# Attention and FP8 feed-forward block: a slot table in place of staged iterations, with row maxima led by half a batch and shift rows sent in quarters

## What is computed

```python
B, T, D, H = 8 batches, 512 rows, 256 columns, 16 heads of 16
xn = layernorm(x)
Q, K, V = xn @ W_q.T, xn @ W_k.T, xn @ W_v.T
Q, K = rope(Q), rope(K)
scores = einsum('bhqd,bhkd->bhqk', Q, K) * 16 ** -0.5     # causal mask
heads = einsum('bhqk,bhkd->bhqd', softmax(scores), V)
attn = heads.reshape(b, t, d) @ W_o.T
xq, wq = fake_quant_fp8(xn), fake_quant_fp8(weight)       # one scale for each tensor
out = x + attn + (einsum('bsd,od->bso', xq, wq) + bias)
```

## Time and profile before

| | us |
|---|---|
| median of 3 runs (467.94 to 469.84) | 468.45 |
| the profiled execution | 468.62 |
| its span from first to last instruction | 466.9 |
| PE busy (share of the span) | 405.5 (87%) |
| DVE busy | 350.1 (75%) |
| ACT busy | 277.3 (59%) |
| POOL busy | 274.4 (59%) |
| mean granted TensorE clock | 0.938 |

### The profile page before, as it was taken

How to read it: one execution, slowest core, us unless ns; L and a number is a source line. 1 busy time by engine, 2 the same in 40 slices (tenths; PEclk the granted TensorE clock), 3 DMA queues, 4 the chain that set the end, 5 groups by cost and what they waited for, 6 DMA issues and landing times.

```text
span 466.9 us, 9145 instructions
## 1 busy us (share of the span) xinstructions
PE 405.5 (87%) x2819; PEld 222.8 (48%) x2819; DVE 350.1 (75%) x1340; ACT 277.3 (59%) x500; POOL 274.4 (59%) x278
## 2 busy tenths in 40 slices
PE   1790676999889999999999999999999999998975
PEld 1440521364345556654565556555655545643443
DVE  3779899969769977997799778977897878842041
ACT  2742932147765677567666765677567656675850
POOL 2304376636746984698459844985498337226552
PEclk9996555599999999999999999999999999999999
DMA  7826747300483238422851375037504760020021
GB/s 234 257 87 197 159 136 193 81 5 18 143 214 84 69 101 204 131 69 78 216 144 46 93 213 152 32 110 206 158 18 124 194 170 2 4 93 3 1 91 46
DMA packets 37617, 53.43 MB, mean 114 GB/s; under 512 B 5152, under 2 KB 31136, under 8 KB 37536
## 3 DMA queue, kind: packets, MB, share of 16 engines
q1 hardware_dynamic: 37568, 52.84, 40.6%
HBM read 35.78 MB, written 17.04 MB: 113 GB/s over the span
## 4 chain that ended last, share of the span: by engine, by line
PE 44%; POOL 22%; ACT 11%; issue 10%; DVE 8%; DMA 3%; POOLq 1%; SPq 1%; ACTq 0%; DVEq 0%
PE st_ps L842 10%; PE o_ps L922 9%; PE s_ps L860 7%; ACT prob L722 6%; PE m_ps L894 5%; PE m_ps L869 4%; POOL prob L427 4%; POOL rot L259 4%; PE m_ps L798 4%; POOL rot L253 3%; DVE scratch L587 3%; POOL xq L457 3%; POOL parts L263 3%; POOL rot L252 2%; POOL qv L453 2%
## 5 line engine op out<-in xcount | busy, mean ns | idle before, releaser
L587 DVE CUSTOM_DVE_ANT_0 scratch<-s_ps,causal 128x512 bf16<-128x512 f32 (+3 forms) x512 | 220.9, 485 | 55.0 <-PE s_ps L860 52.9
L722 ACT ACTIVATE prob<-st_ps 128x512 f32<-128x512 f32 x320 | 174.8, 600 | 97.9 <-PE st_ps L842 97.4
L427 POOL TENSOR_SCALAR_AFFINE_SELECT prob<-prob 128x512 f32<-128x512 f32 (+1 forms) x160 | 86.4, 544 | 130.9 <-ACT prob L722 129.4
L860 PE MATMUL s_ps<-k_st,q_st 96*128 96x512 bf16 (+3 forms) x512 | 130.8, 320 | 7.0 <-DVE rowmax L587 3.2
L842 PE MATMUL st_ps<-q_st,k_st 98*128 98x128 bf16 (+3 forms) x512 | 121.9, 303 | 4.2 <-ACT prob L722 2.8
L922 PE MATMUL o_ps<-prob,v_sb 128*17 128x512 f32 (+3 forms) x1024 | 87.4, 437 | 10.0 <-ACT heads L737 5.1
L842 PEld LDWEIGHTS st_ps<-q_st,k_st 98*128 98x128 bf16 x512 | 42.0, 97 | 76.3 <-ACT prob L722 42.3
L860 PEld LDWEIGHTS s_ps<-k_st,q_st 96*128 96x128 bf16 x512 | 48.9, 99 | 43.7 <-DVE rowmax L587 20.6
L922 PEld LDWEIGHTS o_ps<-prob,v_sb 128*17 128x17 f32 x1024 | 20.5, 96 | 48.3 <-issue 36.0
L587 DVE DVE_READ_ACCUMULATOR2_ANT rowmax<- 128x1 f32 x512 | 41.7, 81 | 0.1
L894 PE MATMUL m_ps<-wo_sb,attnT 128*128 128x256 f32 x128 | 33.2, 381 | 1.8 <-DVE x_res L610 1.4
(11 more groups left out here) (99 smaller groups left out, 502.6 us busy)
## 6 DMA issues: line engine op xcount, KB each, us to landing
qk_parts<-parts SPq DMA_DIRECT2D x16, 768.0 KB, 3.7
q_st<-qk_parts SPq DMA_DIRECT2D x32, 192.0 KB, 3.3
k_st<-qk_parts SPq DMA_DIRECT2D x32, 192.0 KB, 3.7
q_st<-x_dram SPq DMA_DIRECT2D x8, 512.0 KB, 5.5
q_st<-qk_parts SPq DMA_DIRECT2D x32, 128.0 KB, 3.4
k_st<-qk_parts SPq DMA_DIRECT2D x32, 128.0 KB, 3.7
x_res<-x_dram SPq DMA_DIRECT2D x8, 512.0 KB, 3.5
out_dram<-x_res SPq DMA_DIRECT2D x8, 512.0 KB, 4.8
```

The lines of the kernel that those rows point to most:

```text
L427: eng.affine_select(out=ap, in_=ap, compare_op=ALU.is_ge, fill=0.0, base=0, pattern=pat, channel_multiplier=-1).then_inc(masked, 1)
L587: eng.tensor_tensor_reduce(scratch[:, at, col:col + w], s_ps[at][:, col:col + w], causal[:, T - w:T], 1.0, NEG, ALU.add, ALU.max, rowmax[: ...
L722: eng.activation(prob[u][:, half * T:(half + 1) * T], st_ps[ST_BANK[2 * s + half]][:, :], ACT.Exp, scale=SCALE).then_inc(exp_done, 1)
L860: mm = eng.matmul(bank[:, col:col + (qb + 1) * P], q_st[0:ROWS, 1 - par, h, qb * P:(qb + 1) * P], k_st[0:ROWS, 1 - par, h, 0:(qb + 1) * P] ...
```

## The change

The iterations with their stages are replaced by one loop over slots from -10 to 175, which each engine walks with offsets of its own. Batch n has its exponents in slots 20n to 20n + 19 and its maxima ten slots ahead of them, where it was twenty. The list `MISC` becomes the dictionary `OFFSETS` (projections of batch n at slots 20n - 30, -28, -26 and -24, outputs from 20n + 23 to 20n + 34). Each piece of the shift rows now covers one group of four heads: four `shift_rows` for a batch, due in slots 0, 5, 10 and 15. The input is loaded into `xnT` itself and normalised there, in place. Before slot -10 only batch 0 is projected; batch 1 is projected, and batches 3 to 7 are turned, in slots -10 to -4. The last store goes out in four pieces.

```diff
-MISC = [(0, "mt", 1), (0, "v", 0), (1, "qk", 0), (2, "qk", 1), (3, "v", 1), (4, "qk", 2), (5, "o", 0),
-        (6, "o", 1), (6, "qk", 3), (7, "o", 2), (8, "o", 3), (9, "at", 0), (10, "at", 1), (11, "mt", 0),
...
+LEAD = 10
+OFFSETS = {("v", 0): 0, ("mt", 1): 1, ("v", 1): 2, ("o", 0): 23, ("o", 1): 24, ("o", 2): 25, ("mt", 2): 6, ("o", 3): 26,
+           ("at", 0): 26, ("at", 1): 27, ("fin", 0): 28, ("at", 2): 29, ("fin", 1): 30, ("qk", 0): -30, ("mt", 3): 11,
+           ("at", 3): 31, ("fin", 2): 32, ("qk", 1): -28, ("qk", 2): -26, ("fin", 3): 34, ("qk", 3): -24, ("mt", 0): -4}
...
+def quant_slot(n):
+
+    return 23 if n == 0 else SLOTS * n + 16
...
-        turn_ps = [[st_ps[0], st_ps[1]], [s_ps[2], o_ps]]
+        turn_ps = (st_ps[0], o_ps)
...
         @block.sync
...
-            def iteration(b, par, stages, before):
-                if 3 in stages:
-                    shift_rows(b, par, 1)
...
-                if 1 in stages:
-                    query_stacks(b + 2, par, 3 in stages)
-                if 2 in stages:
-                    shift_rows(b + 1, 1 - par, 0)
-                if 1 in stages:
-                    key_stacks(b + 2, par, 3 in stages)
...
+            def shift_rows(n, g):
+
+                c = NG * n + g
+                eng.wait_ge(shift_done, c + 1)
+                eng.dma_start(shift_dram[c % 2].rearrange("t a n -> a t n"), shift[:, :, :])\
+                   .then_inc(shift_out[c % 2], 16)
+                eng.wait_ge(shift_out[c % 2], 16 * (c // 2 + 1))
+                eng.dma_start(q_st[ROWS:ROWS + SHIFT, n % 2, g * HG:(g + 1) * HG, :],
...
+            for slot in range(FIRST_SLOT, END_SLOT):
+                for off, g in ((-3, 0), (2, 1), (7, 2), (12, 3)):
+                    n = batch_at(slot, off)
+                    if n is not None:
+                        shift_rows(n, g)
+                n = batch_at(slot, -22, 1)
+                if n is not None:
+                    query_stacks(n)
+                n = batch_at(slot, -17, 1)
+                if n is not None:
+                    key_stacks(n)
+                n = batch_at(slot, 37 - SLOTS)
+                if n is not None and n > 0:
+                    store(n - 1)
+                n = batch_at(slot, 21)
+                if n is not None:
+                    load_residual(n)
...
         @block.gpsimd
...
-                        if s in (7, 13):
-                            low(eng, n, s // 13)
-                        if s in (3, 8):
-                            rotate(eng, n, s // 8)
-                        if s in (5, 10):
-                            remainder(eng, n, s // 10)
...
+            remainder(eng, 0, 0)
+            invert(2)
+            low(eng, 0, 0)
...
+                for off, step, w in ((-27, rotate, 0), (-25, remainder, 0), (-23, low, 0),
+                                     (-22, rotate, 1), (-20, remainder, 1), (-18, low, 1)):
...
+                for n in quant_at(slot, 2):
...
+                for n in quant_at(slot, 4):
...
         @block.tensor
...
-                    if u == 0 and g % 2 == 0:
-                        eng.wait_ge(shift_in[g // 2], 16 * (b + 1))
...
+                if u == 0:
+                    c = NG * n + g
+                    eng.wait_ge(shift_in[c % 2], 16 * (c // 2 + 1))
```

More of the change, by code:

```diff
@@ L231, in attention_ffn_block @@
         reader = {"qk": (roped, 4), "v": (v_copied, 2), "o": (normed, 4), "at": (at_copied, 4),
[L232 to L239, removed]
+                  "fin": (fin_done, 4), "mt": (shift_done, 4)}
@@ L470, in _ @@
+            nw = NC * D
+            invert(0)
+            invert(1)
+            eng.wait_ge(ln_rstd, 4)
+            fill_ones(0)
+            eng.wait_ge(consts, 7)
+            remainder(eng, 0, 0)
+            invert(2)
+            low(eng, 0, 0)
+            split_weights(0)
+            split_weights(1)
+            split_x(1)
+            for n in range(3, 7):
+                invert(n)
             eng.memset(v_sb[:, :, :, :], 1.0).then_inc(consts, 1)
[L471 removed]
@@ new lines, in high_x, with exp @@
+            def high_x(n):
+                wait_past(eng, full["qk"], 4 * n if n > 1 else 0)
+                eng.copy(x_parts[:, 0], xnT[:, n]).then_inc(x_high, 1)
+            def exp(n, s):
+                g, u = divmod(s, 5)
+                if n > 0 or g > 0:
+                    eng.wait_ge(pv_done, 12 * n + 3 * (g - 1) + (1, 1, 2, 2, 3)[u])
+                for half in range(2):
+                    eng.wait_ge(st_full, 2 * (SLOTS * n + s) + half + 1)
+                    eng.activation(prob[u][:, half * T:(half + 1) * T], st_ps[ST_BANK[2 * s + half]][:, :],
+                                   ACT.Exp, scale=SCALE).then_inc(exp_done, 1)
@@ L974, in _, with scores @@
-            run(iteration)
+            def scores(n, s, between):
+                g, u = divmod(s, 5)
+                if u == 0:
+                    c = NG * n + g
+                    eng.wait_ge(shift_in[c % 2], 16 * (c // 2 + 1))
+                for half in range(2):
+                    i = 2 * s + half
+                    wait_past(eng, exp_done, HALVES * n + ST_BEFORE[i] + 1)
+                    for j, kb, col in unit_parts(u, half):
+                        h = g * HG + j
+                        mm = eng.matmul(st_ps[ST_BANK[i]][:, col:col + T - kb * P],
+                                        k_st[0:ROWS + SHIFT, n % 2, h, kb * P:(kb + 1) * P],
+                                        q_st[0:ROWS + SHIFT, n % 2, h, kb * P:T], start=True, stop=True)
+                    mm.then_inc(st_full, 1)
+                    if half == 0:
+                        between()
```

954 lines of the change are left out of this document (454 added, 500 removed).

## The result

The changed kernel takes **548.09 us** (median of 4 runs, 546.63 to 549.61), the kernel before 468.6 beside it (467.94 to 469.84): a ratio of **1.169, 95% interval 1.164 to 1.174**. The prediction was 534 with a range of 486 to 552 and 0.88 for slower. The profiled execution is one of 549.61 with a span of 547.9.

A forecast was written before the change was run, and what follows sets the result against it. PE bound full batches before; now a wait loop through POOL and SP: slot 10 of batch 0 at 105, batch 1 at 159, five loops of 59.5 to 456.5, end 532.5, plus 1.7: 534 us, range 486 to 552.

The forecast's parts named there:

- The start: Before slot 0: less work ahead of PE's first maximum, slot 0 at 75 against 89.8, a gain of about 15 us.
- The loop: Chain from PE's slot 10 through POOL's `low`, SP's key reads and the third quarter to the next slot 10: 59.5 us.
- (g): PE's clock: each batch restarts at half speed after the wait, costing half of up to 5.7 us, taken as 1.9.
- (c): POOL's ordered work from `low` through rotation, `qv`, remainder, `xq` and the keys' `low`, with five masks: 16.7 us.
- (e): Third quarter's first hop, SBUF to DRAM, directly behind 18 reads: 4.8 us, with 1.4 as bound.
- (f): Third quarter's second hop, DRAM to `q_st`: taken as 2.0 us, with bounds 1.4 and 4.8.
- Hidden wait: Rival: the third quarter lands before PE reaches slot 10, so batches keep their pace: 454 us, chance 0.10.
- Short first hop: Rival: the third quarter's first hop takes 2.0 instead of 4.8, loop 56.7: 514 us, chance 0.12.
- POOL keeps up: Rival: POOL starts the keys' `low` 33 us after slot 10 instead of 40.7, loop 52: 489 us, chance 0.10.
- Clock stays up: Rival: PE's clock stays up in stalls of 8 us, saving 1.9 seven times: 521 us, chance 0.07.
- Late start: Rival: the start isn't earlier than 85, as slots -9 to -5 chain ACT, PE and POOL: 544 us, chance 0.05.
- The signs I named: Seven PE waits for shift rows of 5 us or more, half clock after each, one SP chain, slot 0 near 75.

The follow-up runs named there:

- the cure: Changed kernel with the third quarter of the shift rows sent after the first six key reads instead of behind all 18: 492.65 us, ratio 1.049.
- the best version: Changed kernel plus third quarter between reads, later quantised input, turn and ACT key rounding, some largest values ahead of slot -10, batch 0's input sooner: 464.8 us, 0.992.

## Why the prediction was right

The path, step by step: what I had, and what the changed kernel has.

| point | predicted | measured |
| --- | --- | --- |
| first maximum (slot -10) | 47 | 46.98 |
| slot 0 | 75 | 70.30 |
| slot 10 of batch 0 | 105 | 99.92 |
| slot 10 of batch 1 | 159 | 160.59 |
| slot 10 of batch 6 | 456.5 | 468.02 |
| slot 10 of batch 7 | 501 | 514.31 |
| end of the span | 532.5 | 547.9 |

**The start** was right in kind and 4.7 us too long. From slot -10 to slot 0 it took 23.3, not 28. I had charged ACT's 3.2 us to each of five slots, 16 us; it took 12.2, from 52.17 to the end of the last copy at 64.34, since the first two of the five batches were normalised before slot -10:

```profile
39.30 4.04 ACT L667 ACTIVATE xnT<-xnT,shift_x,rstd 128x256 f32<-128x256 f32 x8 [2.07 <-POOL shift_x L417]
52.17 0.59 ACT L674 COPY xnT<-st_ps 128x512 f32<-128x512 f32 x1 [8.83 <-PE o_ps L788]
...
63.75 0.59 ACT L674 COPY xnT<-o_ps 128x512 f32<-128x512 f32 x1
```

```profile
47.00:70.30 23.30, 18.24 (x98) 12.02 (x98) 19.63 (x79) 12.92 (x24) 11.88 (x9) 0.92 0.36 78
```

PE's clock was also higher (0.92 in this window) than the 0.50 at which the maxima of batch 0 ran before; what that gave isn't shown. The gain is 19.5 us on 89.80.

**The loop** closed where I said, at slot 10, through the same engines in the same order:

| step | predicted | measured |
| --- | --- | --- |
| (a) and (g): PE slots 10 to 16, with the clock | 20.1 + 1.9 | 22.99 |
| (b) to POOL's `low` | 2.0 | 2.35 |
| (c) POOL | 16.7 | 17.33 |
| (d) key write, 18 reads | 3.7 + 8.2 | 4.31 + 8.24 |
| (e) first hop | 4.8 | 4.96 |
| (f) second hop | 2.0 | 1.50 |
| sum | 59.5 | 61.68 |

The choice that mattered was (e). The one row with a shift transfer behind 18 reads the earlier trace rows was taken over the quiet one, and it was right to 0.2; (f) was right to be near the quiet end. SP's hop is 1.35 with a quiet queue, 3.1 behind 6 reads and 4.96 behind 18, and what is in flight decides. The 2.0 us that the Trainium skill (DMA: Bandwidth & Descriptors, Anatomy of one DMA) gives for GpSimd's path would have made 514, and is none of these three.

**Mis-sized terms.** The clock (g): I had 1.9 of a possible 5.7 / 2. The first matmul after each of the seven waits in slot 10 takes 0.61, where the same one takes 0.38 at 70.30, so the clock was down after every one. The clock stays at its lower level from before PE's restart at 345.38 until 351, and slot 10 takes 7.37 (283.70 to 291.07) for 0.89 + 1.08 + 1.49 + 0.99 = 4.45 of work at full clock, 2.9 more: the bound itself. The denser load didn't raise it sooner. With the key write (4.3 for 3.7), POOL (0.6) and slot 17 (0.35), less 0.5 for the second hop, that is the 2.2 of this turn; the five turns together were 9.9 over.

The turn from batch 0 to 1 was put at 54 and took 60.67. It closed over the same chain, and 5.1 of the 6.7 stand in POOL's stretch, from the queries' `low` at 122.74 to the end of the keys' at 142.32: 19.6, where the prediction's terms give 14.5. POOL waited there for exponents ahead of two masks, 2.13 us at 130.27 and 3.25 at 134.15:

```profile
134.15 0.41 POOL L446 TENSOR_SCALAR_AFFINE_SELECT prob<-prob 128x256 f32<-128x256 f32 x1 [3.25 <-ACT prob L697]
```

ACT in its turn waited 3.84 us for PE's scores ahead of 128.71, and PE had stopped twice for the largest values, ahead of 123.20 and 125.84 (1.75 and 1.07), with its clock at 0.66 from 125 to 130. ACT also had the weights' scaling in front of the next exponents (three steps from 130.00 to 132.07). I had costed that batch by what POOL leaves out, and overlooked what waits for the largest values, of which DVE takes three in this turn and five before it; how the 5.1 divides between PE's stops and ACT isn't settled. The rest is in the first two steps of the chain, 22.8 to the start of POOL's stretch, where the prediction's terms give 20.8; the second hop was 0.5 shorter than I had it.

From slot 10 of batch 6 to slot 10 of batch 7 it took 46.3 for 44.5, and from there to the end 33.6 for 31.5: 3.9 more.

So an error below (5.1 us by slot 10 of batch 0, nearly all of it at the start) and three above (6.7, 9.9, 3.9) make +15.4. That they offset is luck: with the start as I had it, the same loop would have ended near 553, just past the range.

**The rivals.** *Hidden wait*: fell; PE waited 44.8 us. *Short first hop*: fell at 4.96. *POOL keeps up*: fell; the keys' `low` starts 40.5 after slot 10 (283.70 to 324.23), where I had 40.7 and the rival 33. *Clock stays up*: fell at 0.50. *Late start*: fell; slot 0 stands at 70.30.

**The signs I named** stood in the profile, with two differences of size: six waits of the seven are over 5 us and the one of batch 1 is 2.82; slot 0 is at 70.3 and not 75.

What I hadn't seen is what the cure showed. With the loop open a batch in the middle of the run still took 52.4, then 48.6, then 47.9, each time for an order of two steps within one engine's queue (DVE's maxima behind the quantised input, a turn behind a bank, exponents behind a rounding). Of the 19.5 us gained at the start, 4 are left in the best version. Its profile (span 460.5 against 466.9) shows where the rest went, counted from slot 0 of a batch to slot 0 of the next: batch 0 takes 47.7 for 42.7 before, batches 1 to 5 together 4.1 more than before, batch 6 44.3 for 41.4, and from slot 0 of batch 7 to the end it takes 56.3 for 54.9. So two thirds of it go in batch 0 and from batch 6 on, outside the full batches. In batch 7 the changed order has ten slots of maxima and the kernel before none; what batches 0 and 6 are made of wasn't tested.

## What to carry to other kernels

A wait moved into a queue is late by all that stands ahead, and where what stands ahead depends on the waiting engine, the lateness repeats each round: follow the chain until it comes back to its start, sum it, and compare with the engine's own period. A small transfer that an engine waits for belongs ahead of bulk reads or between them; giving it another engine's queue gave 16.5 us of the 79 here, and moving it ahead of 12 of the reads gave 55. When work ahead of a phase goes, see what ran under its cover: here eight reductions of DVE turned up in the next phase.

## What the runs showed of the hardware

- **A small DMA behind bulk reads** ends about when they have drained. In the changed kernel the first hop (issued 338.92) ends at 343.88, with the DMA share at 0.82 in 341 to 343 and at 0.00 after; 1.16 us of further issues ahead moved its end by 0.6 only. From another engine's queue it took 4.1 as well.
- **A VectorE step beside a GpSimd step** takes 2.57 us in the version with the third quarter between the reads, and 2.58 in four of eight batches of the changed kernel; in the kernel before all eight take 0.68 to 0.70 (row below). It ends 0.55 after the other's end, so it seems to have waited for nearly all of it. The Trainium skill (SBUF — State Buffer, Who interferes with whom) says that `tensor_scalar` can take the port pair that VectorE shares with GpSimd, and that whichever comes second blocks for the whole instruction. These rows agree, and they have GpSimd first by 0.11.

```profile
L640 DVE TENSOR_SCALAR qe<-qv x8: 683/684/695, 141.8 to 449.4; 128x1024 uint32<-128x1024 uint32 x8
```

- **TensorE's clock** fell to its lower level some 2 us after PE stopped (338.92, and 0.51 in 341 to 343) and came back some 6 us after PE restarted (345.38, and 0.85 in 351 to 352), though PE was busy nearly all of that time. A stop of 2.70 us was enough for a fall in the version with the third quarter between the reads, when PE was back at work already:

```profile
280.00:283.00 3.00, 0.30 (x4) 0.21 (x3) 2.97 (x7) 0.80 (x2) 3.00 (x3) 1.00 1.00 333
283.00:287.00 4.00, 3.91 (x13) 2.52 (x11) 2.99 (x16) 2.03 (x3) 4.00 (x4) 0.57 0.54 175
```

- **A clock of 0.95** in place of 1.00 stood in one profile and in none of the others (that of the version with the third quarter between the reads and the quantised input later); open.
